# Block attention with transposed scores: longer runs of score products between the other matmuls, the normalisation moved on VectorE, and the adding of probabilities in pieces on GpSimd

## What is computed

```
q, k, v = heads of x @ W + b            # 16 heads of width 32, 4 sequences of 512
ctx   = softmax over a 256-wide window around each block of 128 queries
idx   = first token, last token and the 62 tokens with the largest |q|, per head
g_ctx = softmax(q[idx] @ k.T / sqrt(32)) @ v      # those rows see every key
ctx[idx] = g_ctx
```

## Time and profile before

| | us |
|---|---|
| median of 3 runs | 1063.64 (1061.74 to 1065.39) |
| the profiled execution | 1063.53, its span 1061.8 |
| PE busy | 936.7 (88%) |
| DVE busy | 763.1 (72%) |
| ACT busy | 596.2 (56%) |
| POOL busy | 515.0 (49%) |
| L891 DVE reduce of S products, x240 | 148.8 busy, 54.6 idle before |
| L691 POOL add, x30 | 137.2 busy, 110.6 idle before |
| L863 ACT exponential, x256 | 135.7 busy, 67.0 idle before |
| L743 PE S products (q_more), x160 | 68.7 busy, 9.6 idle before |

### The profile page before, as it was taken

How to read it: one execution, slowest core, us unless ns; L and a number is a source line. 1 busy time by engine, 2 the same in 40 slices (tenths; PEclk the granted TensorE clock), 3 DMA queues, 4 the chain that set the end, 5 groups by cost and what they waited for, 6 DMA issues and landing times. The chain is left out here.

```text
span 1061.8 us, 18013 instructions
## 1 busy us (share of the span) xinstructions
PE 936.7 (88%) x5112; PEld 718.2 (68%) x5112; DVE 763.1 (72%) x1347; ACT 596.2 (56%) x913; POOL 515.0 (49%) x458
## 2 busy tenths in 40 slices
PE   5899998799999999965999999992987999999980
PEld 4677886444544444425888888991876899888870
DVE  3425554777777787648887888854777899999984
ACT  3443211567676767744444444441766888888863
POOL 3450000355555556636565555633243576567734
PEclk9999999799999999986999999997998999999995
DMA  7466500634342425202111111122697444334467
GB/s 259 159 221 217 196 1 2 149 89 105 74 117 61 119 61 143 97 28 82 51 53 61 60 59 59 50 70 73 205 282 236 79 77 72 77 72 78 79 159 228
DMA packets 80883, 115.72 MB, mean 109 GB/s; under 512 B 15680, under 2 KB 37056, under 8 KB 80832
## 3 DMA queue, kind: packets, MB, share of 16 engines
q1 hardware_dynamic: 67760, 93.32, 29.0%
q0 software_dynamic: 9760, 20.49, 10.1%
q10 hardware_dynamic: 3312, 1.32, 0.5%
HBM read 74.77 MB, written 40.31 MB: 108 GB/s over the span
## 5 line engine op out<-in xcount | busy, mean ns | idle before, releaser
L1864 DVE TENSOR_TENSOR we_lo<-w_all,we_hi 128x1408 fp32r<-128x1408 f32 (+1 forms) x117 | 192.3, 1672 | 11.6 <-ACT we_hi L1796 10.9
L691 POOL TENSOR_TENSOR pair_sum<-probs 128x2048 f32<-128x2048 f32 x30 | 137.2, 4575 | 110.6 <-ACT probs L863 110.6
L891 DVE TENSOR_REDUCE maxima<-ps_s 128x8 f32<-128x512 f32 x240 | 148.8, 683 | 54.6 <-PE ps_s L743 54.4
L1796 ACT ACTIVATE we_hi<-w_all 128x1408 fp32r (+1 forms) x117 | 165.8, 1420 | 36.7 <-PE e_ps_y L1937 19.9
L863 ACT ACTIVATE probs<-ps_st 128x512 f32<-128x512 f32 x256 | 135.7, 601 | 67.0 <-PE ps_st L801 65.2
L1768 POOL DMA_INDIRECT x_dram<-e_y,who x39 | 99.3, 2547 | 124.5 <-ACT e_y L1813 77.4
L1534 PE MATMUL ps_gu<-sw_hi,x2T_hi 128*128 128x352 f32 (+1 forms) x256 | 88.1, 344 | 2.1 <-issue 1.7
L1534 PE MATMUL ps_gu<-sw_lo,x2T_hi 128*128 128x352 f32 (+1 forms) x256 | 84.0, 328 | 0.0
L1534 PE MATMUL ps_gu<-sw_hi,x2T_lo 128*128 128x352 f32 (+1 forms) x256 | 83.8, 327 | 0.0
L743 PE MATMUL ps_s<-k_more,q_more 96*128 96x512 f32 x160 | 68.7, 434 | 9.6 <-DVE maxima L891 7.8
L1762 POOL DMA_INDIRECT xg<-x_dram,who x39 | 68.4, 1753 | 14.3 <-issue 11.4
(11 more groups left out here) (268 smaller groups left out, 2486.3 us busy)
## 6 DMA issues: line engine op xcount, KB each, us to landing
qk_dram<-qk_ctx SPq DMA_DIRECT2D x32, 512.0 KB, 2.9
q_more<-qk_dram SPq DMA_DIRECT2D x60, 128.0 KB, 3.0
k_more<-qk_dram SPq DMA_DIRECT2D x60, 128.0 KB, 3.1
w_all<-in_L_ffn_w_gate_dram SPq DMA_DIRECT2D x8, 704.0 KB
w_all<-in_L_ffn_w_up_dram SPq DMA_DIRECT2D x8, 704.0 KB
q_first<-qk_dram SPq DMA_DIRECT2D x36, 128.0 KB, 3.1
k_first<-qk_dram SPq DMA_DIRECT2D x36, 128.0 KB, 3.3
x_tile<-in_x_dram SPq DMA_DIRECT2D x16, 256.0 KB, 2.7
```

Source lines behind the costliest of these rows:

```text
L691: pool.tensor_tensor(pair_sum[:, h], probs[:, 2 * h], probs[:, 2 * h + 1], ALU.add).then_inc(added, 1)
L891: dve.tensor_reduce(by_tile[:, t, j, 1:9], bank(p, x).rearrange("p (g n) -> p g n", n=S // 8), axis=AX.X, op=ALU.max).then_inc(s_reduced, 1)
L1796: act.activation(w_hi[kind][:], raw(base, kind), ACT.Copy).then_inc(s[kinds[kind] + "_hi"], 1)
L1864: dve.tensor_tensor(w_lo[kind][:], raw(base, kind), w_hi[kind][:].bitcast(F32), ALU.subtract).then_inc(s[kinds[kind] + "_lo"], 1)
```

## The change

Five edits, all in `attend`:

1. The groups move: `weigh(u-1, 3)` and `sums(u-1, 0)` from step 3 to step 5; `sums(u-1, 1)` from step 7 to step 11, ahead of `weigh(u, 0)`; `back(u-1)` from step 11 to step 15, behind `turn(u+1)`. ScalarE's two copies move along (behind exponentials 5 and 11).
2. The bank that `back` uses comes behind the S products 0 to 4 of unit u+2 in the round of banks; waits of S products are renumbered to fit (S product 5 is now the first of the round, S product 7 waits for the reciprocal of `normalise`).
3. VectorE reduces S products 0 to 4 of unit u+2 ahead of `normalise(u-1)`.
4. GpSimd adds each half in four pieces of 128 x 512, each as soon as its own exponential is done.
5. `bar_u` is gone, with its copy on GpSimd and the wait for it; VectorE reads the kept bar itself.

```
         def bank(p, x):
-            return ps_s[:, (RING * p + x) % BANKS, :]
+            at = x - EARLY if x >= EARLY else x - EARLY - 1
+            return ps_s[:, (RING * (p - 1) + at) % BANKS, :]
 
         def rows_bank(p):
-            return bank(p, NU)[:, 0:TT * HPG].rearrange("p (t j) -> p t j", j=HPG)
+            return ps_s[:, (RING * p + NU) % BANKS, 0:TT * HPG].rearrange("p (t j) -> p t j", j=HPG)
...
-                    pool.wait_ge(turn_ready, u + 1)
-                    pool.tensor_copy(bar_u[:], c.bar[:, :, bass.ds(HPG * (u + 1), HPG)]).then_inc(bar_taken, 1)
                     for h in range(2):
-                        pool.wait_ge(exp_done, NU * u + 2 * HPG * (h + 1))
                         need(pool, sums_done, 2 * (u - 1) + h + 1)
-                        pool.tensor_tensor(pair_sum[:, h], probs[:, 2 * h], probs[:, 2 * h + 1], ALU.add).then_inc(added, 1)
+                        for j in range(HPG):
+                            pool.wait_ge(exp_done, NU * u + 2 * HPG * h + HPG + j + 1)
+                            last = pool.tensor_tensor(pair_sum[:, h, j], probs[:, 2 * h, j], probs[:, 2 * h + 1, j], ALU.add)
+                        last.then_inc(added, 1)
...
-                    if x < 2:
+                    if EARLY <= x < EARLY + 2:
                         need(pe, s_reduced, NU * u + x - 1)
-                    elif x == 2:
+                    elif x == EARLY + 2:
                         need(pe, recip_done, u - 2)
...
-                        if s == 3 and not first:
+                        if s == 5 and not first:
                             weigh(u - 1, 3)
                             sums(u - 1, 0)
-                        if s == 7 and not first:
-                            sums(u - 1, 1)
                         if s == 11:
                             if not first:
-                                back(u - 1, (p + 1) % SLOTS, NU * U if last else NU * (u + 1) + 14)
+                                sums(u - 1, 1)
                             weigh(u, 0)
                         if s == 15:
                             if not last:
                                 turn(u + 1, p)
+                            if not first:
+                                back(u - 1, p, NU * U if isinstance(u, int) and u > U - 3 else NU * (u + 2) + 3)
                             weigh(u, 1)
                             weigh(u, 2)
...
-                        if s == 3 and not first:
+                        if s == 5 and not first:
                             take_out(u - 1)
-                        if s == 7 and not first:
+                        if s == 11 and not first:
                             take_sum(u - 1)
...
-                    if not first:
-                        normalise(u - 1, (p + 1) % SLOTS)
-                    if last:
-                        last_pairs(1)
                     if not (isinstance(u, int) and u > U - 3):
                         for x in range(EARLY):
                             reduce(u + 2, (p + 2) % SLOTS, x)
+                    if not first:
+                        normalise(u - 1, p)
                     if last:
-                        normalise(u, (p + 2) % SLOTS)
+                        last_pairs(1)
+                        normalise(u, (p + 1) % SLOTS)
```

More of the change, by code:

```diff
@@ L609, in attend @@
         turn_in = m.sb("turn_in", [P, TT * (P + 1) + 4], BF16)
-        bar_u = m.sb("bar_u", [P, TT, HPG])
         ps_s = m.ps("ps_s", [P, BANKS, S])
@@ L625, in attend @@
         o_taken, sum_taken = m.sem("o_taken"), m.sem("sum_taken")
-        bar_taken = m.sem("bar_taken")
         built = m.sem("constants_built")
         def bank(p, x):
-            return ps_s[:, (RING * p + x) % BANKS, :]
+            at = x - EARLY if x >= EARLY else x - EARLY - 1
+            return ps_s[:, (RING * (p - 1) + at) % BANKS, :]
         def rows_bank(p):
-            return bank(p, NU)[:, 0:TT * HPG].rearrange("p (t j) -> p t j", j=HPG)
+            return ps_s[:, (RING * p + NU) % BANKS, 0:TT * HPG].rearrange("p (t j) -> p t j", j=HPG)
         def st_bank(p, s):
@@ L663, in _ @@
             def _(pool):
-                pool.tensor_copy(bar_u[:], c.bar[:, :, 0:HPG]).then_inc(bar_taken, 1)
                 pool.memset(c.before[:], 1.0).then_inc(built, 1)
@@ L828, in unit @@
                         sums(u, 1)
-                        back(u, (p + 2) % SLOTS, NU * U)
+                        back(u, (p + 1) % SLOTS, NU * U)
                 pe.sem_inc(s_done, NU)
@@ L901, in step @@
                         dve.wait_ge(row_step, 6 * u + k[0])
+                    bar = c.bar[:, :, bass.ds(HPG * u, HPG)]
                     dve.wait_ge(s_reduced, NU * u + NU)
-                    dve.wait_ge(bar_taken, u + 1)
                     dve.tensor_reduce(m_win[:].rearrange("p t j -> p t j"), windows, axis=AX.X, op=ALU.max)
                     step(dve.tensor_reduce(m_all[:], by_tile, axis=AX.X, op=ALU.max))
-                    step(dve.tensor_tensor(m_bar[:], m_all[:], bar_u[:], ALU.add))
+                    step(dve.tensor_tensor(m_bar[:], m_all[:], bar, ALU.add))
                     step(dve.tensor_tensor(m_row[:], m_bar[:], m_win[:], ALU.max))
@@ L913, in row_maxima @@
                     k[0] += 1
-                    step(dve.tensor_copy(bar_rows, bar_u[:]))
+                    step(dve.tensor_copy(bar_rows, bar))
                     dve.sem_inc(turn_ready, 1)
```

## The result

| | before | after |
|---|---|---|
| median, us | 1063.21 (7 runs, 1061.03 to 1065.39) | 1056.42 (7 runs, 1050.34 to 1060.05) |
| ratio | | 0.9922, interval 0.9900 to 0.9943 |
| the profiled execution, its span | 1063.53, 1061.8 | 1055.94, 1054.2 |

The change makes the kernel 0.8% faster, a difference that the interval keeps apart from nothing. The forecast was 1053 with a range of 1045 to 1062.

What follows compares the result with a forecast made beforehand. TensorE's own list of starts was taken to bound the attention: 0.90 us less per unit, times 13, is 11.7, less end and fill losses 10.8; 1063.53 - 10.8 = 1052.7, stated as 1053, range 1045 to 1062.

Steps and rivals of the forecast that it cites:

- What bounds: Self attention: TensorE's own list of starts sets the time, and what is gained there counts one for one.
- The wait of the row maxima, the 0.80 at S product 3: VectorE's L905, ready at 4.48, waits for GpSimd's fourth add until 5.3; TensorE's S product 3 loses 0.80 us.
- The unit, 16.27 foreseen: One attention unit on TensorE, runs plus groups, takes 16.27 us, 0.90 less than 17.17.
- with the shorter way into the group that follows, 0.03 each: TensorE's runs of six: waits at S products 0 and 10 for reductions cost only 0.03 us each.
- Unit 14, 0.8 for a collision: In unit 14 ST product 12 comes about 0.3 earlier, so L909 meets GpSimd's second half; some 0.8 us lost.
- Normalise: VectorE's moved `normalise` beside GpSimd's second half: any wait lies between nothing and 1.28 us, covered by 1.4 slack; nothing taken.
- the reading of the bar: A register instruction on VectorE, spent inside the row maxima's wait: costs nothing, 0.1 us at most without that wait.
- the removed copy: Copy and wait removed on GpSimd: 0.2 us there, worth nothing, as GpSimd is busy only 107 of 187 us.
- B: Rival: the ports do not bind and the row maxima's wait shrinks or goes; 1043 to 1050 us, chance 0.13.
- C: Rival: VectorE's reductions lag in runs of six, so it nets to nothing; 1060 to 1063 us, chance 0.08.
- Rival A: Second collision: L909 also waits for a GpSimd add of the second half; unit 17.9, about 1073 us, chance 0.19.
- The margin of 0.35: Gap of 0.35 us between L909's start at 5.8 and GpSimd's second half at 6.15; closing it brings the second collision.

Runs made afterwards that it cites:

- Experiment 3: The changed kernel with GpSimd's fourth add of the first half held back until the row maxima have signalled: 1043.61 us, ratio 0.9823.
- experiment 5: The kernel before with the adds in pieces and the fourth add of the first half held back until the row maxima have signalled: 1052.45 us.
- experiment 4: The changed kernel with a 128 x 1024 copy ahead of the adds on GpSimd, so that they start later: 1106.91 us, ratio 1.0415.
- 9: The changed kernel with whole adds again, the first held back until the row maxima have signalled: 1044.59 us, ratio 0.9821.
- 11: The kernel before, adds whole, with only the first add held back until the row maxima have signalled: 1050.50 us, ratio 0.9876.
- experiments 1: The changed kernel with GpSimd's adds whole again, one 128 x 2048 instruction per half: 1105.39 us, ratio 1.039.
- 7: The changed kernel with the fourth add held back, plus three useless VectorE reductions between the row maxima and the next unit's reductions: 1107.16 us, ratio 1.0393.

## Why the prediction was right, and where it wasn't

**What bounds.** Right. The gain in the units is all in the attention, and it shows behind it one for one, as near as 6 us of variation there let one see.

**The wait of the row maxima, the 0.80 at S product 3.** Right, and the step that the sum hung on. With ST product 6 at 383.61 as zero, L905 was ready at 4.47 (foreseen 4.48), four adds, 1.28 long and 1.25 apart, ended at 5.29 (5.3), L905 waited for them (0.86, foreseen 0.8 to 1.0), and S product 3 was held by 0.82 (0.80). Experiment 3 takes the wait away: its run of steps 12 to 15 is 2.37 (299.87 to 302.24) instead of 3.04, and its unit 0.66 shorter.

**The unit, 16.27 foreseen, 16.46 measured.** The step that failed is "with the shorter way into the group that follows, 0.03 each". The prediction put the last S product of a run of six at 2.73 and the group 0.34 behind it, at 3.07. The product came at 2.71 (383.61 to 386.32), but the group 0.43 behind it (386.32 to 386.75). This product is 0.49 long instead of 0.40, as the held ones are. Behind one that was not held, the way into such a group is 0.33 (experiment 5, 298.48 to 298.81). So what a short hold costs ahead of `sums` or `weigh` was mis-sized; only ahead of `turn` does a held product have a way of 0.34 (391.30 to 391.64). So both runs of six are 3.14, which is 2 x 0.07 more than foreseen. The rest is 0.03 at the group of step 15 and 0.02 in the run of steps 12 to 15. Times 13 it is 2.5 us, the largest single part of the 3.2 by which the profiled execution (1055.9) missed the 1052.7 that was worked out for it. The later start (2.1, of which 0.6 is the change's where the prediction had 0.1 for the fill of the first unit) and the low clock (1.7) go the same way. The last units (0.6 gained where 0.8 was charged) and the stretch behind the attention (1.5) go the other. That the sum came within 3.2 is in part luck, since terms of this size cancelled.

**Unit 14, 0.8 for a collision.** Not paid. L909 came there at 438.61 and took 0.23; the second half of the adds began at 438.81, 0.20 behind it and not ahead of it.

**The clock.** It has no term in the prediction, which took the full clock of the earlier trace rows for granted. In the first trace one unit cost 1.7 by it; what set it off there is not shown.

**Normalise, the reading of the bar, the removed copy.** Nothing for each, as foreseen: L919 takes 0.69 beside an add, as L921 did without, and S product 7's wait for the reciprocal never shows.

**The range and the rivals.** B and C are out: L905 waits, and no run of six waits by more than 0.1. Rival A has the mechanism right: 0.7 later adds give exactly its second collision. Its unit of 17.9 is what the two units at the full clock have, but "about 1073" is 34 us short of the 1106.9 measured, since it charges the pause and not the clock behind the pause. The margin of 0.35 was 0.39. Had it been closed, the change would by experiment 4, where the adds are 0.7 later, have been about 4% slower, not 1%.

**What the prediction didn't ask.** It took the five edits as a whole. The pieces alone, which its own rows price (the wait of L907 goes, 0.9 of 17.2), have the better unit (16.26 against 16.46) and the better median (1049.6 against 1053.6 and 1056.4, where 2.6 us come from the units and the rest isn't clear of the variation). The new order gives 0.46 per unit by itself, but it also brings the row maxima forward into the adds, and so its first effect is to turn a gain of 0.9 into one of 0.7. Why it does is in the prediction ("L907 is ready at 4.48, in the middle of the fourth add"); that the adds could as well stand behind it is the next question, and experiments 3, 9 and 11 answer it.

## What to carry to other kernels

Where a short VectorE operation with two SBUF inputs is on the path, don't make the GpSimd work beside it shorter, but give it another place, where its result isn't due yet: one semaphore wait ahead of the add was worth as much as cutting it into pieces (1050.5 against 1049.6), and with the new order 61 us against whole adds without it. Price a pause on TensorE at its length only as long as it is short by the rows of the kernel at hand: a second step, here of 3 us per unit, may lie behind 0.6 us more, so a rival that lengthens a pause needs an end of the range that includes the low clock. And when a change has several edits, price each alone; the best of them may be carrying the others.

## What the runs showed of the hardware that was not expected

TensorE's granted clock falls from 2.4 to 1.2 GHz behind a single pause per unit. It stays there for about 7 us in experiments 1 and 7, and for half of that in the one unit of the changed kernel (325.7 to 329.1), with TensorE busy all the while. In thirteen units of each trace it was low, with S product 3 held by about

- 0.86 (the kernel before): in none;
- 0.82 (the change, two traces): in 1 of 26;
- 1.22: in 1 of 13;
- 1.79 and 1.81: in all 26;
- 2.33: in 11 of 13.

The step from 1.22 to 1.81 costs 43 us on the whole kernel. As 2.33 left units at the full clock and 0.82 had one at the low one, the length of this one pause doesn't settle it alone. Where exactly between them it lies, and what else of the unit it depends on, wasn't tried.

A wait between VectorE and GpSimd is for one instruction at a time: an operation of 16 elements that stood ready got in between two adds that follow each other at once (0.31), and the next one, 0.03 later, waited 1.21 for the second.

GpSimd's add costs 4.57 for 128 x 2048 and 1.28, 1.25 apart, for 128 x 512, so cutting it in four costs 0.45 in all, 10%.
